# Attention over an adjacency matrix with a routed FFN: products two groups behind their transpositions, and all four column groups of P in split halves

## The reference

```python
xl = layernorm(x);  Wh = xl @ W
e = leaky_relu((Wh @ a1)[:, None] + (Wh @ a2)[None, :], 0.2)
P = softmax(where(adj > 0 or on the diagonal, e, -9e15), axis=1)
x1 = x + P @ Wh
t = layernorm(x1);  logits = t @ Wr + br;  two best of 8, their weights from the softmax
out = x1 + sum over the two of weight * (gelu(norm_e(t) @ W1[e] + b1[e]) @ W2[e] + b2[e])
```

## Time and profile before

| | before |
|---|---|
| device time, median of 3 runs | 1056.14 us (1050.57 to 1060.01) |
| profiled execution, its own time | 1057.45 us |
| its span in the trace | 1055.6 us |
| mean granted TensorE clock | 0.968 |
| PE / PEld / DVE / ACT / POOL busy | 91 / 76 / 75 / 58 / 60 % |
| attention stage | 68 to 606 us |
| FFN stage | 640 to 1055 us |

### The profile page before, as it was taken

One profiled execution on the slowest core, in us unless ns is written; L12 is line 12 of the kernel. 1 busy time (PEld: TensorE's weight loads), 2 busy tenths in 40 slices (PEclk: granted clock), 3 DMA queues, 4 the chain that ended last, 5 costly groups with the idle time before them and its releaser, 6 DMA issues.

```text
span 1055.6 us, 23275 instructions
## 1 busy us (share of the span) xinstructions
PE 958.9 (91%) x7614; PEld 806.7 (76%) x7615; DVE 789.8 (75%) x1259; ACT 615.2 (58%) x930; POOL 628.5 (60%) x630
## 2 busy tenths in 40 slices
PE   5948999999999999999999925999999999999994
PEld 4847899889878889887998824777777777777763
DVE  6859998989989899897998442766657566675663
ACT  3667888878788787887876413334343333434341
POOL 2222135285664847638476362578888787888763
PEclk9988999999999999999999957999999999999998
DMA  8165788778788788887885285763223232322221
GB/s 259 13 202 161 267 258 222 233 232 251 247 222 247 215 249 267 227 243 214 241 270 140 87 291 203 247 177 53 49 45 55 41 60 40 50 50 41 42 42 21
DMA packets 92225, 170.82 MB, mean 162 GB/s; under 512 B 19952, under 2 KB 69360, under 8 KB 83824
## 3 DMA queue, kind: packets, MB, share of 16 engines
q1 hardware_dynamic: 57296, 133.00, 38.2%
q0 software_dynamic: 24048, 26.23, 16.1%
q10 hardware_dynamic: 10800, 10.52, 3.3%
HBM read 136.91 MB, written 41.19 MB: 169 GB/s over the span
## 4 chain that ended last, share of the span: by engine, by line
PE 62%; POOL 10%; DVE 8%; ACT 6%; DMA 6%; issue 5%; ACTq 1%; SPq 0%; POOLq 0%; DVEq 0%
PE acc L812 12%; PE tp L796 6%; PE tp L798 6%; PE tp L797 6%; PE acc L815 6%; DMA wsplit_dram<-wsp 5%; PE tp L687 4%; POOL rows_dram L549 4%; PE acc L703 4%; PE acc L704 4%; PE acc L705 4%; PE acc L707 4%; PE tp L656 3%; ACT bias_sb L846 2%; DVE sc L1117 2%
## 5 line engine op out<-in xcount | busy, mean ns | idle before, releaser
L703 PE MATMUL acc<-wh,pt_hi 128*128 128x256 f16 x768 | 211.7, 276 | 22.1 <-DVE pt_lo L1137 22.0
L987 ACT ACTIVATE hf<-tp,b_cols 128x256 f32<-128x256 f32 (+1 forms) x312 | 116.2, 459 | 187.4 <-PE tp L798 183.1
L704 PE MATMUL acc<-wh,pt_hi 128*128 128x256 f16 x768 | 211.6, 276 | 0.0
L705 PE MATMUL acc<-wh,pt_lo 128*128 128x256 f16 x768 | 211.5, 275 | 0.0
L619 POOL DMA_INDIRECT out<-y_sb,yidx x71 | 120.7, 1700 | 94.4 <-DVE y_sb L1386 44.2
L812 PE MATMUL acc<-w_sb,h_hi 128*128 x568 | 170.9, 379 | 5.1 <-issue 3.8
L796 PE MATMUL tp<-x_hi,w_sb 128*128 128x256 f16 (+1 forms) x624 | 162.1, 265 | 2.4 <-DVE x_lo L1358 2.4
L798 PE MATMUL tp<-x_down,w_sb 128*128 128x256 f16 (+1 forms) x624 | 162.1, 265 | 0.0
L509 POOL TENSOR_TENSOR x_late<-x_late,wsp 128x1024 f32<-128x1024 f32 x32 | 114.1, 3566 | 80.4 <-DMA x_late<-in_L_ffn_W 46.9
L797 PE MATMUL tp<-x_lo,w_sb 128*128 128x256 f16 (+1 forms) x624 | 161.7, 264 | 0.0
L1117 DVE SCALAR_TENSOR_TENSOR sc<-t_row,s_col 128x2048 f32<-128x2048 f32 x64 | 154.0, 2432 | 0.0
(11 more groups left out here) (175 smaller groups left out, 1789.0 us busy)
## 6 DMA issues: line engine op xcount, KB each, us to landing
adj_sb<-in_adj SPq DMA_DIRECT2D x64, 1024.0 KB, 7.7
x_late<-in_L_ffn_W SPq DMA_DIRECT2D x32, 512.0 KB, 9.8
wsplit_dram<-wsp SPq DMA_DIRECT2D x32, 512.0 KB, 8.7
w_sb<-wsplit_dram SPq DMA_DIRECT2D x32, 512.0 KB, 5.6
xs<-rows_dram ACTq DMA_DIRECT2D x32, 260.0 KB, 3.2
wsp<-in_L_ffn_W POOLq DMA_DIRECT2D x32, 256.0 KB, 3.8
x<-in_x SPq DMA_DIRECT2D x32, 128.0 KB, 8.5
out<-x SPq DMA_DIRECT2D x32, 128.0 KB
```

What stands on the lines that cost most here:

```text
L703: pe.matmul(o, pt_hi[g][:, cols], wh[:, j, 0, :], start=(j == 0), stop=False)
L704: pe.matmul(o, pt_hi[g][:, cols], wh[:, j, 1, :], start=False, stop=False)
L705: m = pe.matmul(o, pt_lo[g][:, cols], wh[:, j, 0, :], start=False, stop=False)
```

## The change

It does these things:

- GS becomes 4: the fourth group is split like the others. `wh32`, `pt32` and the float32 matmuls go; `wh` grows by the same bytes. For each tile 8 float32 matmuls become 24 float16 ones, and DVE gets a fourth `p_lo`. In the `Wh` stage DVE makes the low half of 8 more tiles.
- On PE the products of groups 2 and 3 of tile i-1 come after the first two transpositions of tile i, and those of groups 0 and 1 each after the transposition two groups on.
- On DVE `masked(i+1)` stands ahead of `p_lo(i, 0)`, the two halves of `scores(i+2)` are apart, and `p_lo(i, 3)` is last.
- On ACT both `exps` come ahead of `p_hi(i, 2)`, and `w_scaled` and the second `mask` between `p_hi` 2 and 3.
- Router work is later: `normalise` at q = 1, both PE halves at q = 2, DVE's choice of experts at q = 3, `choose_rows` at q = 0 of the next group ahead of `moments1`, and POOL's gates and scatters one tile later and behind `row_scales`.
- SP stores a weight chunk one tile earlier.

```diff
-    GS = G - 1
+    GS = G
@@ SP
-                if e > 0:
-                    store_w(e - 1, q)
+                if i >= 3:
+                    store_w(i - 3)
@@ POOL
             def attend(i):
-                b, q = i // RB - 2, i % RB
+                b, q = (i - 1) // RB - 2, (i - 1) % RB
                 if in_batch(b):
                     if q == 0:
                         gates(b)
                     scatter_rows(b, q)
-                if q == 0 and in_batch(b + 1):
-                    row_scales(b + 1)
                 if i + 1 < T:
                     w_rest((i + 1) // CHUNKS, (i + 1) % CHUNKS)
+                if i % RB == 0 and in_batch(i // RB - 1):
+                    row_scales(i // RB - 1)
...
-            for i in range(T + RB):
+            for i in range(T + RB + 1):
@@ PE
                 if g % 2 == 0:
                     pe.wait_ge(s_e[g // 2], i + 1)
-                if g == 1:
-                    if within(i, 1, T):
-                        pe.wait_ge(s_hi, G * i)
-                elif g > 1 or within(i, 1, T):
-                    pe.wait_ge(s_lo, GS * i + max(g - 1, 0))
+                if g < 2 and i > 0:
+                    pe.wait_ge(s_lo, GS * i + g - 1)
+                if g > 1:
+                    pe.wait_ge(s_lo, GS * i + g - 1)
...
                 if 1 <= i <= T:
+                    av(i - 1, 1 - u, 2)
                     av(i - 1, 1 - u, 3)
-                if in_batch(b) and q in (1, 2):
-                    router_t(b, q - 1)
+                if in_batch(b) and q == 2:
+                    router_t(b, 0)
                 if now:
+                    p_transpose(i, u, 2)
                     av(i, u, 0)
-                if in_batch(b) and q in (1, 2):
-                    router_mm(b, q - 1)
+                if in_batch(b) and q == 2:
+                    router_mm(b, 0)
+                    router_t(b, 1)
                 if in_batch(b) and q == 3:
                     router_pos(b)
                 if now:
-                    p_transpose(i, u, 2)
+                    p_transpose(i, u, 3)
                     av(i, u, 1)
-                    p_transpose(i, u, 3)
-                    av(i, u, 2)
+                if in_batch(b) and q == 2:
+                    router_mm(b, 1)
```

More of the change, by code:

```diff
@@ L417, in _ @@
                     sp.dma_start(b2_rep[:, :], b2.rearrange("(o e) d -> o (e d)", o=1).broadcast_to([P, E * D])).then_inc(s_b2, 16)
-            for q in range(CHUNKS):
-                store_w(E - 1, q)
+            for j in range(T - 3, T):
+                store_w(j)
             def load_chunk(j):
@@ L921, in attend @@
                     mask(i + 2, u, 0)
-                if in_batch(b) and q in (1, 2):
-                    router(b, q - 1)
+                if i + 1 < T:
+                    exps(i + 1, 1 - u, 0)
+                    exps(i + 1, 1 - u, 1)
+                if in_batch(b) and q == 1:
+                    for k in range(RB):
+                        normalise(b, k)
+                if in_batch(b) and q == 2:
+                    router(b, 0)
+                if now:
+                    p_hi(i, 2)
+                    w_scaled(i)
+                if ahead:
+                    mask(i + 2, u, 1)
+                if in_batch(b) and q == 2:
+                    router(b, 1)
+                if now:
+                    p_hi(i, 3)
                 if in_batch(b) and q == 3:
                     gate_exp(b)
-                if ahead:
-                    mask(i + 2, u, 1)
-                if now:
-                    p_hi(i, 2)
-                if i + 1 < T:
-                    exps(i + 1, 1 - u, 0)
-                if now:
-                    p_hi(i, 3)
-                if i + 1 < T:
-                    exps(i + 1, 1 - u, 1)
-                if now:
-                    w_scaled(i)
-                if in_batch(b) and q == 0:
-                    for k in range(RB):
-                        normalise(b, k)
             mask(1, 1, 0)
@@ L1236, in attend @@
                 here = in_batch(b)
+                if ahead:
+                    diagonal(i + 1, v)
                 if behind:
@@ L1239, in attend @@
                 if ahead:
-                    diagonal(i + 1, v)
+                    masked(i + 1, v)
                 if behind:
@@ L1278, in _ @@
                 attend(i)
+            choose_rows(NBATCH - 1)
             dve.wait_ge(s_slot, NBATCH)
```

67 lines of the change are left out of this document (30 added, 37 removed).

## The result

| | before | after |
|---|---|---|
| device time, median | 1057.04 us (1050.57 to 1060.01, 4 runs) | 1080.38 us (1078.89 to 1081.27, 4 runs) |
| profiled execution's span | 1055.6 us | 1079.1 us |
| mean granted TensorE clock | 0.968 | 0.953 |

The changed kernel is slower: the ratio is 1.0247 (95 % interval 1.0215 to 1.0278). The prediction was 1057 us, with a range from 1042 to 1076.

The account below looks back on a forecast made before the run. A chain of waits set the old batch; afterwards DVE and the circle through ACT would. Attention -4.6, drain +1.8, tail +3.5 and Wh stage +0.3 gave +1.0 on 1057.45, 1058.5; less 1.3 for the profiled execution, 1057 us, range 1042 to 1076.

Parts of the forecast that it names:

- DVE passes PE: Attention tile: with a fourth p_lo DVE takes 14.76 us, PE falls to 14.0.
- The stall of 5.11 us: DVE's wait for p_hi once per batch, behind ACT's normalise and POOL's late row scales; claimed to end.
- the circle: Loop of waits through DVE, PE and ACT, from p_lo(3) to the next tile's; claimed to set a batch of 64.5 us.
- The tail: POOL's scales, gates and scatters after attention ends; claimed +3.5 us, all of it showing.
- POOL against DVE: POOL's weight subtraction and DVE instructions holding each other up in attention; 1.1 us taken for each batch.
- rival C: POOL's subtraction meets scores or mask subtraction, 2.1 us per hit; slower, 1071 or 1084 us; chance 0.27.
- 2.9 us of router work: DVE's router work per batch: 1.0 for choose_rows at q = 0, 1.9 for the choice of experts at q = 3.
- 6.5 x (65.6 - 66.3): Attention from tile 6 on, 6.5 batches going from 66.3 to 65.6 us each: -4.6 us.
- the start: Wh stage: 8 more 256-column subtractions on DVE, only the last showing, +0.3 us.
- 14.8 on PE before: First four tiles, without router work: 14.8 us on PE before, 14.8 on DVE after, so 0 difference.
- B: PE is the bound and gives back its 27 us: 1029, or 1034 by DVE's work; chance 0.18.
- D: The stall at normalise goes only in part, POOL's scales still late: up to 5 us a batch, 1089; chance 0.03.

Follow-up runs that it names:

- e2: Changed kernel with POOL's weight subtraction cut from 1024 columns to 8 (low halves of FFN weights left wrong): 1059.83 us, ratio 1.0045.
- e17: e13 with both long PE pauses of a batch filled with transpositions of the identity that nothing reads: 1065.47 us, ratio 1.0106.
- e13: Changed kernel with POOL's row scales first, then its weight subtraction, made to wait for DVE's mask subtraction of the next tile: 1075.02 us, ratio 1.0195.
- e8: Changed kernel with PE's pause at q = 2 filled with 24 identity transpositions that nothing reads: 1075.22 us, ratio 1.0193.
- e5: Kernel before with POOL's weight subtraction cut from 1024 columns to 8 (low halves of FFN weights left wrong): 1042.21 us, ratio 0.9868.
- e4: Kernel before with only the split of the fourth group and a fourth p_lo at the end of DVE's tile, old order kept: 1081.15 us, ratio 1.0245.
- e15: e6 with POOL's row scales ahead of its weight subtraction, which waits for DVE's mask subtraction of the next tile: 1041.68 us, ratio 0.9885.
- e9: Changed kernel with POOL's weight subtraction waiting for DVE's mask subtraction of its next tile, row scales behind it: 1102.63 us, ratio 1.0470.
- e12: e6 with POOL's weight subtraction waiting for DVE's mask subtraction of its next tile, row scales behind it: 1069.26 us, ratio 1.0152.
- e6: Changed kernel with all its order moves, but the fourth group still in float32 and no fourth p_lo: 1053.86 us, ratio 0.9985.

## Why the prediction was wrong

**Right.** DVE passes PE: plain tiles took 14.90 for the forecast 14.76. The stall of 5.11 us is gone. PE waits for `p_lo(3)` ahead of the second transposition, up to 2.9 us. DVE waits at q = 1 for `p_hi(2)`, 1.37 us where about 2 was said. DVE is busy 62.54 of 66 us, just under the 95 % named. The tile lengths of the circle hold where nothing meets and the clock is whole. From e2 (q = 1, 3 and 0) and e17 (q = 2), which show each of them undisturbed:

| tile at | q = 1 | q = 2 | q = 3 | q = 0 | batch |
|---|---|---|---|---|---|
| forecast | 16.5 | 15.5 | 16.7 | 15.8 | 64.5 |
| undisturbed | 16.75 | 16.0 | 16.62 | 15.78 | 65.15 |
| changed kernel | 17.07 | 16.62 | 18.61 | 15.97 | 68.27 |

The tail was right as well, +2.9 for +3.5; behind it came 1.5 us that I had at nothing.

**Wrong 1, PE's pauses: they had no price.** The forecast said that PE would wait for `p_lo(3)`, and its sum holds nothing for that. But the clock falls at these pauses, and PE's next matmuls, one each 0.21 us instead of 0.11, are then late for DVE. e13 against e17 shows it without meetings on scores or mask subtraction: 67.50 - 65.93 = **1.57 us for each batch**, 1.33 at q = 2 and 0.24 at q = 3. That is the price in e13, whose clock fell at q = 2 in four batches of five. In the changed kernel it fell there in two, and the tile is 16.62 - 16.0 = 0.62 over the undisturbed one. With the 0.24 at q = 3 (an estimate, taken over from e13) the clock costs the changed kernel some **0.9 us a batch**; e8, with one of the two pauses filled, got back 0.81. No rival held this step.

**Wrong 2, the term "POOL against DVE": 1.1 for each batch was too little.** In the changed kernel's trace, between the ninth row sum and the 29th, nine half scores are longer than undisturbed, by 0.29 to 1.75 us, and three `gap_l` by 1.0: 10.5 us in all, **2.1 us for each batch**. With the clock's 0.9 that is 3.0 of the 68.27 - 65.15 = 3.1. The mask subtraction, which rival C named beside the scores, is not hit (mean 4432 ns, 4425 in e13); small instructions that work on SBUF alone are (`gap_l`, mean 905 ns against 158 before). Each hit costs what is left of POOL's instruction when DVE comes, and not the whole 2.1: in the earlier trace rows 327.36 + 2.14 - 327.71 = 1.79 for the 1.66 measured. The kernel before had a second hit in the very batch that was read, so its 2.9 us of router work held 0.86 of a meeting. This `lg` takes 0.19 undisturbed, and in all five batches it took 1.05 or 2.06:

```profile
316.86 1.05 DVE L1181 TENSOR_TENSOR lg<-lg,b_r_rep 128x32 f32<-128x32 f32 x1
```

Nor had I counted what meetings cost before: 1.25 in each batch and 5.4 ahead of the first row sum (e5). e2 got back 2.8 for each batch, more than the meetings, because with them the long pause at q = 3 went, and the clock fell after one of five long pauses at q = 2.

The two terms, 3.1 for the 1.1 forecast, and the 0.65 that the circle was short make the 2.7 by which the batch was missed: 13.4 us over five batches.

**Wrong 3, the sum "6.5 x (65.6 - 66.3)".** It took the first batch for one like the others. It went from 63.18 to 69.37, **+6.2 for -0.7**, 6.9 us of the miss. 2.7 of them are the miss of every batch. 3.1 come from the kernel before, whose first batch was shorter than the later ones (63.18 for 66.27): the scales had no gates and no scatter ahead of them, and DVE's stall was 3.03 us and not 5.11.

```profile
162.34 2.36 DVE L1137 SCALAR_TENSOR_TENSOR pt_lo<-tp,pt_hi 128x1024 f16<-128x1024 f32 x2 [3.03 <-ACT pt_hi L884]
```

The last 1.1 is the changed kernel's first batch over its later ones; the clock fell at both of its long pauses. The four tiles ahead of it (+1.7 for 0) and the start (+1.4 for +0.3) add 2.8: "14.8 on PE before" was measured at 14.5. Together 13.4 + 6.9 + 2.8, less 1.7 for the part after the batches and 0.6 for the tail, plus the 1.5 behind it, is 22.3 of the 22.5 us.

**The rivals.** C named the result nearest, 1084 for two hits more. That is luck in good part: the meetings came out 1.0 us a batch over the 1.1 taken, not 4.2, and under the 1.5 from which C was to decide. Its mechanism is there, as the larger part of the 3.1; the clock, the short circle and the first batches made up the rest of the loss. B is refuted: the saving of PE, 27 us, never came up in the time, as the split alone (e4) has a ratio of 1.0245, and e15 against e17, both without meetings on scores or mask subtraction and without a fall of the clock in the five batches, gives 65.93 - 62.35 = 3.6 us for each batch in favour of no split. D is refuted: ACT did not wait for `nb` in the changed kernel; it did in e9, where POOL was held up.

**What stays open.** Why the clock falls after one pause of 2.54 us and not after the next like it. How the loss at q = 3 (1.99 us over the undisturbed tile) divides between clock and meetings in the changed kernel, since no run takes away one there and leaves the other as it was. And where 1.5 us behind the last scatter come from.

## What to carry to other kernels

Work moved off the fuller engine onto the next one pays only up to the point where that one becomes the bound; from there, its stalls, however short, are all on the path, and stalls that lay under another wait must be priced anew. An engine that becomes the one that waits is not free either: look at the granted clock behind each pause that a change brings, and price matmuls there by rows at the lower clock. Before a new wait goes into an in-order list, read down the list what stands behind it: the same timed subtraction, in the order alone, cost 15 us (e12 against e6) and, with the row scales ahead of it, gave 12 (e15 against e6).
